# A conv kernel with a five-step diffusion: both divergences on TensorE, and a new order of the work that makes the coefficients

## What is computed

```python
s = group_norm(x)                                  # 32 groups of 2 channels
g, g1 = relu(bn(dwconv3x3(s, wg))), relu(bn(dwconv3x3(s, wg1)))
gy, gx = sobel(s)
Dx, Dy = 1 / (gy*gy/4 + 1), 1 / (gx*gx/4 + 1)
ux = 0.5*(roll(g, 1, w) - roll(g, -1, w));  vy = 0.5*(roll(g1, 1, c) - roll(g1, -1, c))
Ax, Ay, Bx, By, E = g*DT, g1*DT, Dx*DT, Dy*DT, (ux + vy)*DT
D = 1 / (1 + 2*Bx + 2*By)
for _ in range(5):     # h0: the state before the last
    h, h0 = D*((1-2*Bx-2*By)*h0 - 2*E*h + (2*Bx-Ax)*roll(h,1,w) + (2*Bx+Ax)*roll(h,-1,w)
               + (2*By-Ay)*roll(h,1,c) + (2*By+Ay)*roll(h,-1,c)) + 2*DT*D*s, h
x = x + relu(bn(h))
x = x + relu(conv3x3(group_norm(x), alpha*ternary(W)) + b)
```

## Time and profile before

| | us |
|---|---|
| median of 3 runs | 327.84 (327.47 to 328.92) |
| the profiled execution, its own time | 327.07 |
| its span in the profile | 324.1 |
| DVE busy | 270.0 (83%) |
| PE busy | 254.3 (78%) |
| ACT busy | 129.1 (40%) |

### The profile page before, as it was taken

One profiled execution on the slowest core, in us unless ns is written; L12 is line 12 of the kernel. 1 busy time (PEld: TensorE's weight loads), 2 busy tenths in 40 slices (PEclk: granted clock), 3 DMA queues, 4 the chain that ended last, 5 costly groups with the idle time before them and its releaser, 6 DMA issues.

```text
span 324.1 us, 5181 instructions
## 1 busy us (share of the span) xinstructions
PE 254.3 (78%) x2252; PEld 228.0 (70%) x2252; DVE 270.0 (83%) x224; ACT 129.1 (40%) x198; POOL 7.2 (2%) x25
## 2 busy tenths in 40 slices
PE   0125779999887999997008999999999987788794
PEld 0114569797776996686008999998998977776683
DVE  1896343499899999579999999999999999997921
ACT  3235569905671252512002244152351150451943
POOL 1000000000000000001000001011010000000000
PEclk9999986557995589999656999999999999799999
DMA  7540000000000000000600003361951003000033
GB/s 255 167 157 0 0 0 5 1 2 2 0 2 2 2 2 0 0 2 0 129 0 2 0 2 65 67 129 18 231 111 35 1 0 131 0 2 0 0 129 129
DMA packets 5173, 14.44 MB, mean 45 GB/s; under 512 B 2336, under 2 KB 2336, under 8 KB 4128
## 3 DMA queue, kind: packets, MB, share of 16 engines
q0 software_dynamic: 720, 5.24, 8.0%
q1 hardware_dynamic: 4144, 8.16, 7.7%
q10 hardware_dynamic: 288, 0.72, 0.7%
HBM read 6.79 MB, written 2.10 MB: 27 GB/s over the span
## 4 chain that ended last, share of the span: by engine, by line
DVE 34%; PE 12%; issue 3%; ACT 1%; DVEq 0%; ACTq 0%
DVE ring L796 21%; PE psum L1048 5%; PE psum L1121 4%; DVE first_two L872 3%; DVE stats L809 2%; PE psum L956 2%; DVE coef L839 2%; DVE coef L804 1%; DVE coef L755 1%; DVE coef L771 1%; DVE first_two L576 1%; DVE coef L850 1%; ACT coef L325 0%; DVE lo L845 0%; DVE mv L812 0%
## 5 line engine op out<-in xcount | busy, mean ns | idle before, releaser
L796 DVE TENSOR_TENSOR ring<-coef,state 128x2048 f32<-128x2048 f32 x51 | 113.5, 2290 | 6.2 <-ACT state L325 5.1
L1048 PE MATMUL psum<-mats,ring 128*128 128x128 f32 x816 | 96.0, 277 | 7.0 <-DVE ring L796 6.9
L1048 PEld LDWEIGHTS psum<-mats,ring 128*128 128x128 f32 x816 | 90.9, 143 | 10.6 <-DVE ring L796 10.2
L325 ACT ACTIVATE state<-psum 128x1024 f32<-128x1024 f32 x36 | 35.1, 1024 | 94.2 <-PE psum L1048 60.0
L1007 PEld LDWEIGHTS psum<-coef,state 32*128 32x128 f32 x768 | 36.1, 289 | 2.0 <-issue 2.0
L1007 PE MATMUL psum<-coef,state 32*128 32x64 f32 x768 | 36.8, 378 | 0.0
L1048 PE MATMUL psum<-mats,first_two 128*128 128x128 f32 x144 | 20.7, 306 | 18.6 <-DVE first_two L576 18.6
L576 DVE SCALAR_TENSOR_TENSOR coef<-coef 128x2048 f32<-128x2048 f32 x15 | 34.4, 2291 | 0.4
L1048 PEld LDWEIGHTS psum<-mats,first_two 128*128 128x128 f32 x144 | 19.0, 161 | 18.9 <-issue 18.8
L325 ACT ACTIVATE coef<-psum 128x512 f32<-128x512 f32 (+1 forms) x22 | 17.2, 792 | 33.6 <-PE psum L1007 21.4
L985 PE MATMUL psum<-hi_s,sobel_m 128*128 128x512 f32 (+2 forms) x48 | 21.1, 443 | 7.0 <-DVE lo_s L638 5.8
(11 more groups left out here) (123 smaller groups left out, 265.1 us busy)
## 6 DMA issues: line engine op xcount, KB each, us to landing
first_two<-coef POOLq DMA_DIRECT2D x5, 1024.0 KB, 7.1
coef<-in_x SPq DMA_DIRECT2D x2, 1024.0 KB, 5.8
coef<-in_wide_taps SPq DMA_DIRECT2D x4, 384.0 KB, 4.2
ring<-in_x SPq DMA_DIRECT2D x2, 512.0 KB, 6.4
ring<-in_x SPq DMA_DIRECT2D x1, 1024.0 KB, 9.0
out<-coef SPq DMA_DIRECT2D x2, 512.0 KB, 3.1
out<-coef SPq DMA_DIRECT2D x4, 256.0 KB, 2.5
mats<-in_matrices ACTq DMA_DIRECT2D x1, 384.0 KB, 6.1
```

The source lines that it names most:

```text
L325: return nc.scalar.activation(dst, src, func, **kw)
L796: V.tensor_tensor(wc(ring[:, slot, :]), wc(coef[:, t, a, :]), h_at(t, k, dw, dc), ALU.mult)\
L1048: ins = mm(slot_ap(name)[:, (j % 8) * 128:(j % 8) * 128 + 128], src[:, j * 128:j * 128 + 128], ident, is_transpose=True, start=first and j ...
```

## The change

It rewrites the head; steps and tail stay, but for signs (`A0`, the sources and the products have the other sign, which ACT turns when it takes a sum, so that the divergence needs no -1) and the order of the five products within a step. Part by part:

1. Tile 0's divergence goes to PE too (`divergence(0, h)`), after `depthwise(1, 0)`; tile 1's comes right behind `depthwise(1, 1)`, ahead of all steps.
2. The four neighbour coefficients are still six DVE operations per tile, in another form (`over_rows`, `over_channels`, `other_rows`, `other_channels`); those of tile 1 stand ahead of `step(1, 0)`, not behind.
3. ACT's `reorder` is gone: `scale_grouped` on DVE writes the scaled and grouped `s` in one pass, ahead of `scale_s`. ACT's `split_hi(1)` goes to DVE.
4. `centre`, `square_of` and `sum_squares` go by halves.
5. Order: `wsum` and the threshold before the Sobel sums, `ternary` right after tile 1's squares; `var_1` after tile 0's four Sobel halves, which now stand together; `depthwise(0, 0)` and `(0, 1)` stand together behind them. Taps are loaded earlier, into three places.

```diff
+            for q in range(2):
+                sp.dma_start(taps_at[q][:, 0:4 * 6 * W], wide_taps[q]).then_inc(taps_in[q], 16)
             sp.dma_start(x_in[1], x_nat[1]).then_inc(x_loaded[1], 16)
             for k in range(2):
                 sp.dma_start(wl[64 * k:64 * k + 64, :].rearrange("i (k o) -> i k o", o=C),
                              conv_w.rearrange("y x i o -> i (y x) o")).then_inc(wl_in, 16)
...
             def square_of(t):
-                act.wait_ge(xm_ready, t + 1)
-                copy(wc(square), h_at(t, 0), ACT.Square).then_inc(sq_ready, 1)
+
+                if t:
+                    act.wait_ge(vsum_ready, 2)
+                for h in range(2):
+                    act.wait_ge(xm_ready, 2 * t + h + 1)
+                    copy(wc(half(square, h)), h_at(t, 0, w0=h * W // 2, w1=(h + 1) * W // 2), ACT.Square)\
+                        .then_inc(sq_ready, 1)
 
...
-            def reorder(t):
-
-                act.wait_ge(s_ready, t + 1)
-                copy(s_grouped[t].rearrange("p (g a w) -> p w a g", a=CP, w=W),
-                     h_at(t, 0).rearrange("p w (a g) -> p w a g", g=CG)).then_inc(s_reordered, 1)
...
+            scale_taps(range(0, 5))
             rsqrt_first(128, GROUPS)
-            scale_taps(range(0, 4))
-            reorder(0)
-            scale_taps(range(4, 6))
-            sobel_square(0, 0, 0)
-            square_of(1)
-            sobel_square(0, 0, 1)
+            act.wait_ge(wl_in, 32)
+            copy(wabs, wl, ACT.Abs, accum_out=wred[:, 0:1]).then_inc(wabs_ready, 1)
+            scale_taps(range(5, 8))
             to_depthwise(0, 0)
             to_depthwise(0, 1)
...
+            wrap(0, 0, s_halo)
+            scale_taps(range(8, 10))
+            square_of(1)
+            sobel_square(0, 0, 0)
+            sobel_square(0, 0, 1)
             sobel_square(0, 1, 0)
             sobel_square(0, 1, 1)
-            scale_taps(range(6, 8))
-            act.wait_ge(wl_in, 32)
-            copy(wabs, wl, ACT.Abs, accum_out=wred[:, 0:1]).then_inc(wabs_ready, 1)
-            split_hi(1)
-            scale_taps(range(8, 12))
-            reciprocal_first(0)
-            scale_taps(range(12, 16))
-            reorder(1)
+            scale_taps(range(10, 16))
+            rsqrt_first(128, GROUPS)
             to_natural(0, 0)
             to_natural(0, 1)
-            wrap(0, 0, s_halo)
+            reciprocal_first(0)
             to_natural(0, 2)
             to_natural(0, 3)
-            d_of(0)
-            for g in range(2):
-                for h in range(2):
-                    sobel_square(1, g, h)
             to_depthwise(1, 0)
             to_depthwise(1, 1)
+            act.wait_ge(s_ready, 2)
+            wrap(1, 0, s_halo)
+            for g in range(2):
+                for h in range(2):
+                    sobel_square(1, g, h)
             wait_reader(act, "gx_1_0")
             wait_reader(act, "gx_1_1")
             copy(coef[:, 1, 2, :], coef[:, 1, 1, :], bias=(1.0 + 2 * DT) * S).then_inc(shifted_ready, 1)
-            wrap(1, 0, s_halo)
+            d_of(0)
+            reciprocal_first(1)
...
+            def scale_grouped(t):
+
+                dve.wait_ge(xm_ready, 2 * t + 2)
+                rs = gsum[:, t, 3, :].rearrange("p (a g) -> p a g", a=CP).unsqueeze(3).unsqueeze(4)
+                V.tensor_tensor(s_grouped[t].rearrange("p (g e a w) -> p a g e w", e=2, a=CP, w=W),
+                                h_at(t, 0).rearrange("p w (a g e) -> p a g e w", a=CP, e=2),
+                                rs.broadcast_to([128, CP, CG // 2, 2, W]), ALU.mult).then_inc(s_grouped_ready, 1)
+
+            def scale_s(t):
                 s = grouped(h_at(t, 0))
-                leave(f"var_{t}")
+                dve.wait_ge(s_grouped_ready, t + 1)
                 signal(V.tensor_tensor(s, s, over_w(gsum[:, t, 3, :]), ALU.mult), s_ready, t + 1)
 
...
-            split_lo(0)
+            ask_scale(0)
+            sum_x(1, 1)
+            rsqrt(128, GROUPS, gsum[:, 0, 3, :])
+            scale_grouped(0)
             mean_of(1)
-            centre(1)
-            sum_squares(1)
-            scale_s(1)
-
...
+            threshold()
+            scale_s(0)
+            split_hi(0)
+            split_lo(0)
+            centre(1)
+            sum_squares(1)
...
+
                 then(V.tensor_scalar(wtern, wabs, wred[:, 1:2], None, ALU.is_gt))
...
-            def diffusivities(t):
-
-                c = [coef[:, t, i, :] for i in range(NCOEF)]
-                then(stt(c[4], c[1], S, c[3], ALU.add, ALU.mult))
-                then(stt(c[5], c[0], S, c[3], ALU.add, ALU.mult))
-                signal(V.tensor_tensor(c[2], c[4], c[5], ALU.add), sb_ready, t + 1)
-
-            def divergence(t):
+                then(stt(coef[:, t, 5, :], coef[:, t, 0, :], S, coef[:, t, 3, :], ALU.add, ALU.mult))
+
+            def both_diffusivities(t):
+
+                signal(V.tensor_tensor(coef[:, t, 2, :], coef[:, t, 4, :], coef[:, t, 5, :], ALU.add), sb_ready, t + 1)
+
...
                     wait_reader(dve, f"cv_{t}_{q}")
-                g, g1, e, e1 = wc(gN[t]), wc(g1N[t]), wc(coef[:, t, 3, :]), wc(coef[:, t, 2, :])
-                V.tensor_tensor(e[:, 1:W - 1, :], g[:, 0:W - 2, :], g[:, 2:W, :], ALU.subtract)
-                V.tensor_tensor(e[:, 0, :], g[:, W - 1, :], g[:, 1, :], ALU.subtract)
-                then(V.tensor_tensor(e[:, W - 1, :], g[:, W - 2, :], g[:, 0, :], ALU.subtract))
+
...
+            def over_rows(t):
+
+                taken_out(t)
+                dve.wait_ge(d_ready, 2 * t + 1)
+                then(stt(coef[:, t, AXM, :], gN[t], 2.0, coef[:, t, 0, :], ALU.mult, ALU.mult))
+                stt(coef[:, t, AXP, :], coef[:, t, AXM, :], -0.5, coef[:, t, AXP, :], ALU.mult, ALU.add)\
+                    .then_inc(axp_ready, 1)
...
             def divergence_taken(t):
 
-                dve.wait_ge(d_ready, 2 * t + 2)
+                dve.wait_ge(d_ready, 2 * t + 1)
+                wait_job(dve, f"dv_{t}_1")
                 for h in range(2):
                     name = f"dv_{t}_{h}"
-                    wait_job(dve, name)
-                    frees(stt(half(coef[:, t, AE, :], h), slot_ap(name), -1.0, half(coef[:, t, 0, :], h), ALU.mult,
-                              ALU.mult), name)
+                    frees(V.tensor_tensor(half(coef[:, t, AE, :], h), slot_ap(name), half(coef[:, t, 0, :], h), ALU.mult),
+                          name)
+
+            def source(t):
+
                 for h in range(2):
                     wait_reader(dve, f"dv_{t}_{h}")
-
...
@@ -872,53 +909,54 @@
                     V.tensor_tensor(wc(first_two[t][:, :]), wc(coef[:, t, A0, :]), h_at(t, k), ALU.mult)\
                         .then_inc(kept_made[t], 1)
 
+            ternary()
+            ask_scale(1)
+            shifted(0)
+            rsqrt(128, GROUPS, gsum[:, 1, 3, :])
             denominator(0)
-            ternary()
+            scale_grouped(1)
+            scale_s(1)
+            split_hi(1)
             split_lo(1)
             newton(0)
-            diffusivities(0)
+            across_columns(0)
+            across_rows(0)
+            both_diffusivities(0)
             wait_job(dve, "alpha")
             then(V.reciprocal(wred[:, 5:6], slot_ap("alpha")[:, 1:2]))
             ins = V.tensor_tensor(wred[:, 7:8], slot_ap("alpha")[:, 0:1], wred[:, 5:6], ALU.mult)
             ins.then_inc(alpha_ready, 1)
             dve.wait_ge(alpha_ready, 1)
             leave("alpha")
-
-            divergence(0)
-            channels_made = over_channels(0)
-            g_made = scaled_g(0)
-            channels_made()
-            g_made()
+            denominator(1)
+            over_rows(0)
+            over_channels(0)
+            other_rows(0)
+            newton(1)
+            other_channels(0)
+            divergence_taken(0)
+            across_rows(1)
             source(0)
-            columns_made = plus_columns(0)
             dve.wait_ge(outp_in, 16 * 10)
             ask_rsqrt(V.tensor_scalar(rs_in[:, 0:1], outp[:, 3:4], BN_EPS, None, ALU.add))
-            columns_made()
...
             first_source(0)
-            denominator(1)
-            columns_made()
+            across_columns(1)
+            both_diffusivities(1)
+
+
+            rsqrt(128, 1, outw[:, 0:1])
+            then(stt(outw[:, 2:3], outw[:, 0:1], -1.0, outp[:, 0:1], ALU.mult, ALU.mult))
+            then(V.tensor_tensor(outw[:, 1:2], outw[:, 2:3], outp[:, 2:3], ALU.mult))
+            signal(V.tensor_tensor(outw[:, 3:4], outp[:, 1:2], outw[:, 1:2], ALU.add), outw_ready, 1)
             step(0, 0)
-            newton(1)
-            diffusivities(1)
-
-
-            rsqrt(128, 1, outw[:, 0:1])
-            then(V.tensor_tensor(outw[:, 2:3], outw[:, 0:1], outp[:, 0:1], ALU.mult))
-            then(V.tensor_tensor(outw[:, 1:2], outw[:, 2:3], outp[:, 2:3], ALU.mult))
```

(56 more changed lines are left out.)

217 lines of the change are left out of this document (109 added, 108 removed), and 7 rows, old and new, of the table early.

## The result

The changed kernel takes **311.11 us** (median of 4 runs, 310.17 to 311.65), the kernel before 328.15 us beside it (4 runs, 327.47 to 328.92). The ratio is 0.948, with a 95% interval of 0.944 to 0.951: 5% faster. Of 25 executions of the kernel before, 21 took 325.9 to 329.2 us and four 320.4 to 323.8, these at a mean clock of 0.910 to 0.918 (0.883 to 0.895 in the 17 others that have it on record), and against the four the changed kernel is 3 to 4% faster. The profiled execution took 310.17 us.

The account below looks back on a forecast made before the run. VectorE's chain in the head was taken as the bound: 21.6 + 126.3 (work) + 13.7 (waits) = 161.6 us to the steady run, against 173.2, so 11.6 less: 315.5 profiled, 316.3 us median, range 312 to 320.5.

Parts of the forecast that it names:

- What bounds the kernel, and the gain from waits alone: Head is a VectorE chain: work hardly changes, 125.9 to 126.3 us; waits fall from 25.7 to 13.7 us.
- The wait at `alpha` and `shifted(1)`: VectorE, from 70.6 us, waits 1.2 us for TensorE's Sobel halves of tile 1, then 1.9 for ScalarE's last square and copy.
- `var_1`: Behind tile 0's four Sobel halves on TensorE; VectorE asks at 39.6 us and has a new wait of 2.5 us.
- rsqrt: VectorE waits 2.4 us for ScalarE's rsqrt of tile 1, since ScalarE scales twelve more taps before it.
- First sum: VectorE's fourth product needs a ring buffer back from TensorE's first sum of step (0,0): new wait 5 to 7 us, taken as 5.7.
- State, `wsum`, square of tile 1: Old VectorE waits in the head of 5.10, 9.24 and 6.24 us, all forecast to go.
- `scale_grouped`: New VectorE operation, run twice: 3.3 us each, between 2.3 and 4.4; 6.6 us for both.
- The clock in the passes, the hinge: TensorE's depthwise passes all run at clock 1.00, 5.59 us each instead of 10.52, as no idling comes right before them.
- the rival that they fall by themselves: Clock falls inside the depthwise passes without a gap: steady run at 172 us, time 326.7; chance 0.14.
- Behind the steady run's start: Steps and tail: an earlier steady run brings the end forward by as much, 11.6 us.
- shorter waits, 310 to 311 us: Rival: `scale_grouped` takes 2.3 us and the clock rises at once; steady run at 155 to 157 us; chance 0.07.

Follow-up runs that it names:

- the run with the early rsqrt: Changed kernel with ScalarE's rsqrt of tile 1 ahead of its last six scalings of taps: 309.93 us.
- The doubled halves: Changed kernel with tile 1's two gx halves of Sobel sums issued twice on TensorE: 315.26 us.
- the gap: Changed kernel with TensorE made to wait before tile 0's first depthwise pass until all taps are scaled, idling 3.84 us: 328.00 us.

## Why the prediction was right or wrong

The mechanism was right, one moment on TensorE was mis-sized, and the sum was 5.3 us too long against the profiled execution (315.5 against 310.17). By its steps:

- **What bounds the kernel, and the gain from waits alone:** right. The work was forecast at 126.3 us and is 125.4, the waits at 13.7 and are 10.3.
- **The wait at `alpha` and `shifted(1)`: the step that failed.** The forecast had 1.2 + 1.9 us, there is none. It had `alpha` start at 59 + 12.1 = 71.1 us; it started at 67.1. Of these 4.0 us, 2.7 are the start of tile 1's four Sobel halves: the forecast let TensorE wait for tile 1's parts until "about 59", but the first matmuls need only the high part, which was there at 56.2, and they began at 56.35 (the low part, there at 58.5, cost a wait of 0.52 us). The other 1.3 us are their length, 10.8 instead of 12.1. The 12.1 us, from the earlier trace rows, have the waits of 1.2 us taken off and still hold a start with the clock at half; at full clock and without waits the four halves take 10.0 us (the run with the early rsqrt). ScalarE's last square and copy, 74 in the forecast, were through at about 70.3, just ahead of VectorE at 70.57. The doubled halves showed the rest: with TensorE 4.3 us later both waits come, and the time is 315.26 us.
- **`var_1`:** 1.04 us instead of 2.5, of the same kind: the four halves of tile 0 began 1.8 us later than forecast but took 10.8 us, 29.78 to 40.57, not 13.5. **rsqrt:** 2.26 and 0.29 us, forecast 2.4. **First sum:** 6.68 us, forecast 5.7 of 5 to 7. VectorE came to its fourth product at 113.0 us instead of 116.6, and TensorE gave the buffer back at 119.7 instead of about 122: both early, for the same reason. **State, `wsum`, square of tile 1:** gone, as said.
- **`scale_grouped`:** 3.98 and 4.00 us, forecast 3.3 of 2.3 to 4.4, so 1.4 us more for both. The sum of the work came out near by luck, since two errors cancel: it was still 0.9 too long, because the small waits of before, about 1.6 us, had been counted as work that stays, and some 0.7 us lie in starts. The rule of the Trainium skill (SBUF — State Buffer, Door 1: The DMA port swizzle) put the operation at the upper end, and it was nearer there: 1.74 times the plain one, with the order of its broadcast in that figure.
- **The clock in the passes, the hinge:** right. 13.2 us of passes and shifts in a row (41.0 to 54.2) kept 1.00, and the rival that they fall by themselves is refuted for this length. What a late TensorE costs was also right: the rival let 11 us of it come through as 10.4 (326.7), and with tile 0's passes at half behind the gap 15.6 us (11.8 and 3.8) came through as 16.9. That 326.7 and the 328.0 measured lie close is luck, since the lateness isn't the same.
- **Behind the steady run's start** the forecast let nothing change, and within the span that was right (150.8 and 150.9 us). The 1.3 us that the sum was too long there lie outside the span, 1.8 us instead of 3.0; no run tells why.
- **The range:** "shorter waits, 310 to 311 us" had a chance of 0.07, tied to `scale_grouped` at 2.3 us. The waits were shorter for another reason, with `scale_grouped` near its upper end. The range below the forecast should have held a case in which TensorE's dense stages run at their full-clock time.

## What to carry to other kernels

A stage's length taken from a trace carries that trace's clock and waits: before it goes into a sum for a new order, recount it from its matmuls at the clock that the new order will have. An operation moved off the busiest engine is worth what the receiving engine has to spare until somebody waits for it: here 0 us, and 7 us once half a divergence had been put behind the first sums. And keep small matmuls from starting behind a gap: look at what gates their first operand.
